# Three stages of layer 0 written as one program each, in a decoder kernel of twelve stages

## The reference, cut to layer 0

```python
x = x + L0_attn(_layernorm(x))
x = x + L0_xattn(_layernorm(x), ctx, ctx, side)       # 16 heads over 64 context tokens
x = x + L0_ffn(_layernorm(x))

def L0_attn(x):
    xn = ln(x, n1)
    br, bi = split(xn @ in_proj.T)                    # 64 each
    c = causal convolution of br + i*bi with mag**n * exp(i*n*frequency)
    out = concat(couple(c.real), couple(c.imag)) @ out_proj.T
    x = x + sigmoid(xn @ gate_w.T + gate_b) * out
    return x + silu(ln(x, n2) @ mlp_w1.T + mlp_b1) @ mlp_w2.T + mlp_b2      # 1024 hidden

def L0_ffn(x):
    tern = lambda w: clip(round(w / mean|w|), -1, 1) * mean|w|
    h = gelu(ln(x, ln1) @ tern(w1).T + b1)            # 1024 hidden
    return ln(h, ln2) @ tern(w2).T + b2
```

## Time and profile before

| | us |
|---|---|
| three runs | 4320.02, 4322.22, 4322.23; median 4322.22 |
| profiled execution, time and span | 4315.53 and 4313.5 |
| start of L0_attn, of L0_xattn, of L0_ffn | 21.7, 281.7, 410.1 |
| start of L1_attn | 632.7 |
| TensorE busy, of the span | 3646.5 (85%) |
| TensorE busy until 632.7 | 452.7 |

### The profile page before, as it was taken

The page is one execution under the profiler, slowest core; times in us unless marked ns, Lnnn a source line. Parts: engine busy times, 40 slices in busy tenths (PEclk is TensorE's granted clock), DMA queues, the critical chain, the costliest instruction groups (busy, mean ns, idle before and its releaser), DMA issues. The chain is left out here.

```text
span 4313.5 us, 51717 instructions
## 1 busy us (share of the span) xinstructions
PE 3646.5 (85%) x17354; PEld 2158.5 (50%) x17354; DVE 2241.4 (52%) x5187; ACT 1391.6 (32%) x2971; POOL 1363.4 (32%) x1971
## 2 busy tenths in 40 slices
PE   5778679799999978688869899999696878996996
PEld 3456447444555557333334454545574344444563
DVE  3346445464564558455536665756323336665443
ACT  2224111243343346122224444444132124441221
POOL 1013014142242326232235444444312134443111
...
DMA packets 48968, 106.99 MB, mean 25 GB/s; under 512 B 6548, under 2 KB 38676, under 8 KB 46420
## 3 DMA queue, kind: packets, MB, share of 16 engines
...
...
## 5 line engine op out<-in xcount | busy, mean ns | idle before, releaser
L2249 POOL TENSOR_SCALAR probs<-probs,inv_sum 128x512 f32<-128x512 f32 x640 | 436.3, 695 | 961.3 <-DVE inv_sum L2370 961.0
L2207 ACT ACTIVATE probs<-psum_banks,neg_max 128x576 f32<-128x576 f32 x640 | 468.6, 737 | 711.4 <-DVE neg_max L2449 711.4
L2449 DVE TENSOR_REDUCE neg_max<-psum_banks 128x1 f32<-128x576 f32 x640 | 454.7, 752 | 192.9 <-PE psum_banks L2082 186.4
L2082 PE MATMUL psum_banks<-keys_T,queries_T 64*128 64x288 f32 x2560 | 406.7, 437 | 40.8 <-ACT probs L2207 28.4
L2379 DVE COPY probs_T<-psum_banks 128x512 f32<-128x512 f32 x640 | 408.8, 680 | 20.0 <-PE psum_banks L2011 20.0
L2082 PEld LDWEIGHTS psum_banks<-keys_T,queries_T 64*128 64x128 f32 x2560 | 225.1, 189 | 267.8 <-ACT probs L2207 162.1
L2011 PE MATMUL psum_banks<-ident,probs 128*128 128x128 f32 x2560 | 351.8, 281 | 3.2 <-POOL probs L2249 2.3
L2011 PEld LDWEIGHTS psum_banks<-ident,probs 128*128 128x128 f32 x2560 | 276.3, 141 | 130.4 <-POOL probs L2249 73.8
L2041 PE MATMUL psum_banks<-probs_T,values 128*64 128x512 f32 x1280 | 307.3, 604 | 2.2 <-issue 2.2
L3950 PE MATMUL psum_banks<-w_L_experts_up,sorted_T 128*128 x552 | 255.8, 600 | 0.4 <-issue 0.3
...
L2445 DVE TENSOR_TENSOR psum_banks<-psum_banks,key_mask 128x128 f32<-128x128 f32 x192 | 57.4, 299 | 244.1 <-PE psum_banks L2082 244.1
...
## 6 DMA issues: line engine op xcount, KB each, us to landing
expert_outputs<-expert_rows SPq DMA_DIRECT2D x92, 128.0 KB, 1.7
group_normed_T<-sorted_rows SPq DMA_DIRECT2D x20, 512.0 KB, 4.1
...
```

Of the source, the lines that this page charges most:

```text
L2082: last = pe.matmul(k.ps[:, 2 * h + a, 0:HALF], qT[r, b % 2, j, t * P:(t + 1) * P], kT[r, j, k0:k0 + HALF], start=True, stop=True)
L2207: act.activation(prob[:, g % PB, h * w:(h + 1) * w].rearrange("p (a n) -> p a n", a=2), k.ps[:, 2 * h:2 * h + 2, 0:HALF], ACT.Exp, bias=nm ...
L2249: pool.tensor_scalar(w, w, inv[:, g % 4, h:h + 1], 1.0, ALU.mult, ALU.mult).then_inc(shared, 1)
L2449: dve.tensor_reduce(nmax[:, g % 4, h:h + 1], k.ps[:, 2 * h:2 * h + 2, 0:HALF], AX.XY, ALU.max, negate=True).then_inc(maxed, 1)
```

## The change

The three stages share one set of weights (`begin_layer0`), which SP loads inside L0_attn, behind what L0_attn itself needs; x comes in four parts, batch 0 in the first block and the others between the weights. The fill moves to SP in L0_ffn. L0_xattn loses its loads and their waits, and keeps its order otherwise.

L0_attn becomes one block without a loop: all banks and buffers are named by batch, most are double, and each engine has one list of steps over the four batches. The rows normed once are scaled on VectorE in four places (`scale_once`); the powers of both norms are one operation of 2 x 4 columns, and GpSimd does those of all batches first. It also adds the bias row and the middle rows to x, 128 x 1024 at a time. The ternary weights are summed and rounded between the last additions of L0_attn.

L0_ffn becomes one block too. up now gives the hidden values transposed (features on partitions), so that Gelu takes the bias, and no transposes back are needed. The second norm is applied behind down: `w2g` is the weight times gain with a column of ones, whose product is the row's sum; ScalarE squares the hidden values, VectorE adds the squares of eight chunks, and one more product sums them. `centre` subtracts the mean's row, GpSimd makes the reciprocal root, `add` scales and adds to x. Two rows (gain's sums, and offset times weight) are made once by `rows()`.

```diff
--- before.py
+++ after.py
+    def load_x(self, sp, b):
+
+        rows = slice(TT * b, TT * b + TT)
+        sp.dma_start(self.x[:, rows, :], self.dram["x"][:, rows, :]).then_inc(self.x_loaded[b], 16)
+
+    def fill(self, sp):
+
+        for g in range(GROUPS):
+            for n in range(0, SORTED, 8):
+                some = min(8, SORTED - n)
+                sp.dma_start(self.sorted_x[g][n * P:(n + some) * P, :].rearrange("(n p) d -> p n d", p=P),
+                             self.zeros[:, :].unsqueeze(1).to_broadcast([P, some, D])).then_inc(self.filled, 16)
...
+    def begin_layer0(self, ctx):
+
+        names = ["L0_xattn_" + n for n in ("wq", "wk", "wv", "wo")] + ["ctx_T_twice", "head_mask8", "L0_side", "L0_ffn_w1",
+                                                                       "L0_ffn_w2"]
+        self.w0 = {n: self.weight(n, ctx) for n in names}
...
 def l0_ffn(k):
...
+                def down(s):
+                    pe.wait_ge(moved, PER * (s + 1))
+                    for t in range(TT):
+                        n = TT * s + t
+                        bank = 4 + t
+                        if s:
+                            pe.wait_ge(centred, n - TT + 1)
+                        elif t < 2:
+                            pe.wait_ge(rows_moved, t + 1)
+                        for j in range(HC):
+                            pe.matmul(ps[:, bank, 0:D + 1], h[:, s % 2, j, t * P:(t + 1) * P], w2g[:, j, :],
+                                      start=j == 0, stop=j == HC - 1)
+                        pe.wait_ge(square_added, (HC - 1) * (s + 1))
+                        pe.matmul(ps[:, bank, D + 1:D + 2], acc[:, s % 2, t * P:(t + 1) * P], k.ones[:, 0:1], start=True,
+                                  stop=True).then_inc(downed, 1)
+
...
+                turn(0)
+                up(0)
+                turn(1)
+                up(1)
+                rows()
+                for s in range(B):
+                    down(s)
+                    if s + 2 < B:
+                        turn(s + 2)
+                        up(s + 2)
...
+                        u = PER * s + KC + j
+                        act.wait_ge(unit_made, u + 1)
+                        if j == 0 and s >= 2:
+                            act.wait_ge(downed, TT * (s - 1))
+                        act.activation(h[:, s % 2, j, :], ps[:, u % 4, :], ACT.Gelu,
+                                       bias=up_bias[:, j:j + 1]).then_inc(moved, 1)
+                        if j:
+                            square(s, j - 1)
+                    square(s, HC - 1)
+
...
+                batch_rstd(0)
+                batch_rstd(1)
+                pool.tensor_copy(b2w[:, :, :], b2.unsqueeze(2).to_broadcast([P, HC, P])).then_inc(columns_made, 1)
+                pool.memset(w2g[:, :, D:D + 1], 1.0).then_inc(columns_made, 1)
...
+                def constant(s):
+                    pool.wait_ge(rows_moved, 2)
+                    pool.wait_ge(normed, TT * (s + 1))
+                    rows = k.x[:, TT * s:TT * s + TT, :]
+                    pool.tensor_tensor(rows, rows, const_row[:, :].unsqueeze(1).to_broadcast([P, TT, D]),
+                                       ALU.add).then_inc(biased, 1)
+
...
+                def centre(n):
+                    bank = 4 + n % TT
+                    dve.wait_ge(downed, n + 1)
+                    dve.tensor_scalar(ms[:, n, :], ps[:, bank, D:D + 2], 1.0 / HID, None, ALU.mult).then_inc(moment, 1)
+                    dve.wait_ge(moment, n + 1)
+                    dve.scalar_tensor_tensor(out=var[:, 0, n:n + 1], in0=ms[:, n, 0:1], scalar=ms[:, n, 0:1],
+                                             in1=ms[:, n, 1:2], op0=ALU.mult, op1=ALU.subtract).then_inc(spread_made, 1)
+                    if n >= 2:
+                        dve.wait_ge(added, n - 1)
+                    dve.scalar_tensor_tensor(out=y[:, n % 2, :], in0=mean_row[:, :], scalar=ms[:, n, 0:1],
+                                             in1=ps[:, bank, 0:D], op0=ALU.mult, op1=ALU.add).then_inc(centred, 1)
+
...
 def l0_attn(k):
...
+                load(angles_loaded, count)
+                load(in_loaded, w_in, gate)
+                k.load_x(sp, 1)
+                load(out_loaded, coup, w_out)
+                load(rows_loaded, k.w0["rows"])
+                k.load_x(sp, 2)
+                k.load_x(sp, 3)
+                load(mlp_loaded, w1, w2)
+                load(ternary_loaded, *ternary)
+                load(others_loaded, *k.side_inputs())
+                sp.wait_ge(others_loaded, 16 * len(k.side_inputs()))
...
+                units_of("turn", 0)
+                pe.wait_ge(in_loaded, 32)
+                beta_and_gate(0)
+                units_of("turn", 1)
+                beta_and_gate(1)
+                couple()
+                pe.wait_ge(out_moved, 2)
+                outputs(0)
...
+                def batch_rstd(s):
+                    n = slice(TT * s, TT * s + TT)
+                    pool.wait_ge(aggr, TT * (s + 1))
+                    pool.tensor_scalar(rs[:, 0, n], mv[:, n, 1], 1.0 + EPS, EPS * EPS, ALU.mult, ALU.add).then_inc(
+                        shift, 1)
+                    pool.tensor_scalar(rs[:, 1, n], mv[:, n, 1], EPS, 1.0, ALU.add, ALU.mult).then_inc(shift, 1)
+                    pool.wait_ge(shift, 2 * s + 2)
+                    pool.tensor_tensor(rs[:, 2:4, n], rs[:, 0:2, n],
+                                       k.half[:, 0:2 * TT].rearrange("p (a n) -> p a n", a=2), ALU.pow).then_inc(rstd, 1)
+
...
+                def abs_sums():
+                    dve.wait_ge(ternary_loaded, 32)
+                    for i, w in enumerate(ternary):
+                        dve.tensor_reduce(asum[:, i:i + 1], w[:, :, :], AX.XY, ALU.add,
...
+                def quantise():
+                    dve.wait_ge(total_made, 1)
...
+                batch_stats(0)
+                reduce_angles()
+                batch_scale(0)
+                batch_stats(1)
+                batch_scale(1)
+                scale_once(0)
+                batch_stats(2)
+                batch_stats(3)
+                finish_tables()
+                rotate(0)
+                dve.wait_ge(rows_loaded, 16)
+                bias_gate(0)
...
+                add(2)
+                abs_sums()
+                quantise()
+                add(3)
+                dve.wait_ge(added, 2 * B)
...
 def l0_xattn(k):
...
-                    for w in what:
-                        whole = tuple(slice(None) for _ in w.src.shape)
-                        sp.dma_start(w.dst[whole], w.src[whole]).then_inc(sem, 16)
-
-                load(keys_loaded, ctx2, wk, mask8)
-                load(queries_loaded, wq)
-                load(side_loaded, logw)
-                load(values_loaded, wv)
-                load(rows_loaded, *k.stage_rows)
...
-                sp.dma_start(k.x[:, :, :], dram["x"]).then_inc(loaded, 16)
                 sp.dma_start(k.vecs[:, :], dram["vecs"]).then_inc(loaded, 16)
                 sp.dma_start(k.ident[:, :], dram["ident"]).then_inc(loaded, 16)
-                sp.wait_ge(loaded, 48)
+                k.load_x(sp, 0)
...
+                        sp.wait_ge(k.x_loaded[b], 16)
...
+            if FIRST > 2:
+                @block.sync
+                def _(sp):
+                    k.fill(sp)
+
+        layer0 = ExitStack()
+        if FIRST < 3:
+            k.begin_layer0(layer0)
```

877 lines of the change are left out of this document (521 added, 356 removed).

## The result

The changed kernel took 4159.8 us (median of four runs, 4153.2 to 4164.3) against 4322.2 for the kernel before (4320.0 to 4325.5): a ratio of 0.9623, 95% interval 0.9606 to 0.9639, so 162.4 us less. The forecast was 4152 with a range of 4143 to 4178, a gain of 170.6 us. The direction and the size are right; the forecast is 7.8 us too low. On two further sets of runs of the same two kernels the ratios on record were 0.9608 (0.9588 to 0.9628; another chip, medians 4190.5 and 4366.0) and 0.9620 (0.9606 to 0.9634; medians 4164.0 and 4324.7); the quotients of these medians are 0.9598 and 0.9628.

What follows compares the result with a forecast made beforehand. L0_attn and L0_ffn were taken as bound by chains between engines with barriers, L0_xattn by busy TensorE. Gains of 16.3 + 72.0 + 3.4 + 78.9 = 170.6 us off 4322.2 gave 4152, range 4143 to 4178.

Steps and rivals of the forecast that it cites:

- Term 1: Entry: waiting only for the small loads, with the fills moved away, starts stage 0 at 5.4 instead of 21.7; gain 16.3 us.
- Batch 0 of x is there: Head of L0_attn: the 512 KB load has landed by 5.4 us, so statistics need no wait and end at 7.2.
- Term 2: L0_attn: one block with another batch's work in each wait takes 188.0 us against 260.0; gain 72.0.
- From there TensorE is never last: L0_attn from outputs(0), 32.0 us after the start: other engines' work hides under TensorE's, which sums to 151.0 us.
- another batch's work in each wait: L0_attn: the new order fills TensorE's waits with other batches' work; part of the 72.0 us gain, not sized alone.
- Term 3: L0_xattn: head no longer waits for a weight load, six semaphores fewer to clear; gain 3.4 us, bounds 2.8 to 4.5.
- Term 4: L0_ffn: transposes, evictions, scaling, ternary rounding and four barriers removed; stage 143.7 us against 222.6, gain 78.9.
- I take it over unchanged: Everything after layer 0: same instructions before and after, so no change in length was forecast.
- (a): Clock: all twelve handovers of the two programs cost a cold start of 2.1 us, adding 25: 4177 us; chance 10%.
- (b): GpSimd's large adds collide with VectorE, which stands still with TensorE behind it, 38.6 us: 4190; chance 7%.
- (c): Entry not freed: loads land behind one another, TensorE starts as late as before, adding 16.3 us: 4168; chance 6%.
- (d): TensorE gets the lower of its two clocks throughout the two programs: 4428 us; chance 3%.

Runs made afterwards that it cites:

- fill_at_entry: Changed kernel with the six fills back in the entry's second block instead of L0_ffn; L0_attn starts at 16.17 us and takes 194.2 for 187.6.
- in_turn: Changed kernel with L0_attn's batches one after another on every engine, instead of interleaved; L0_attn took 249.2 us.

## Why the prediction was right, and where it was off

**Term 1, entry.** Forecast: stage 0 at 5.4, gain 16.3. Measured 4.98, 16.7. The fill's issue was priced right (11.4 for 11), but only as issue; fill_at_entry shows that 6.6 us more hang on its transfers where a load is waited for at once. "Batch 0 of x is there" was wrong: VectorE waited 1.28 us and began at 5.62, which the earlier start made good.

**Term 2, L0_attn.** Forecast 188.0, measured 188.4, 187.6 and 188.3. The head: TensorE's first turn at 12.9, measured 12.38; outputs(0) at 37.4 with some 2 us of waiting for VectorE, measured 37.12 with 2.50. The stage itself began 0.4 us earlier than forecast, so the head was 0.1 us longer than its 32.0. The sum behind it was 151.0 to the last product and 0.9 for the addition; outputs(0) to the end of the last addition is 152.5 (37.12 to 189.64). The end of the block: 4.1, measured 3.77. "From there TensorE is never last" holds: no wait is over 1.6 us. in_turn shows that the step which carried the term, another batch's work in each wait, is worth 61.6 of the 72.4 us between 260.0 and 187.6, and the rest is the head.

**Term 3, L0_xattn.** Forecast gain 3.4 with bounds of 2.8 to 4.5; measured 2.7 by the first profile (128.4 to 125.7). The norm's scaling starts 3.40 us after the stage (196.81) instead of 6.13, as said. VectorE reads the first scores only 2.15 us sooner (18.08 us after the start for 20.23). The half microsecond between goes in the product of the keys, in before and in after:

```profile
291.12 2.69 PE L1104 MATMUL psum_banks<-w_ctx_T_twice,w_L_xattn_wk 128*128 128x256 f32 x8
```

```profile
200.01 3.28 PE L1445 MATMUL psum_banks<-w_ctx_T_twice,w_L_xattn_wk 128*128 128x256 f32 x8
```

It starts earlier in the stage and runs more of its length at half clock, which lasted until 11 us behind the stage's start in before and until 9.4 in after. The end of the block took 3.14 us for 3.56, so 0.4 and not 0.5 for the semaphores. The term was mis-sized by 0.7, for the most part because it had no price for this half clock.

**Term 4, L0_ffn.** Forecast 143.7, measured 144.3, 144.5 and 144.1. Start of up(0): 7.8 after the stage's start, measured 7.7; it took 16.81 where 15.8 stood; up(1) 27.3, measured 27.6; constants 6.9, measured 6.92; a down 14.8, measured 14.72: the product with no row took 0.13 and not 0.25, but the groups of 257 columns 3.48 and 3.57 and not 3.45, so that two small misses cancel; the end 2.5 and 2.3, measured 2.65 and 2.28.

**The sum.** Layer 0 ended at 463.5 (462.8 twice), forecast 462.1. The miss is in the sentence that was no term: "I take it over unchanged". The later layers took 3699 us in the profile for 3681. Over the four runs of each, the median span less layer 0 is 3694.6 for 3687.5, so 7.1 of the 8.2 us by which the gain fell short (162.4 for 170.6), and layer 0 is 1.4 of them. The text did name this as what would make it wrong, but gave it no price. A rate was at hand, as an estimate: with TensorE busy 129.2 us at a clock of 0.83 in L1_attn and 392.8 at 0.80 in L2_attn, a hundredth of the clock is worth 1.6 and 4.9 us there, and both fell to 0.77. That the total came within 8 us is in part luck: the later layers of this kernel moved between 5 us less and 10 more than before's from set to set. The gain of layer 0, 169 to 171 us by the profiles, is not.

**The rivals.** (a) no: every up behind a handover took 13.9 to 14.0 (the first of L0_ffn stands at the head, and was priced cold), and a gap of 2.8 us was still free. (b) the collision, yes, its price on TensorE, no. (c) no. (d) not in these stages; the clock did fall without waits, but in L1_attn, 110 us behind them.
